# A new order in the state-space chunk, and D*u as diagonal matmuls on TensorE

## What is computed

```python
def _mamba(x, ...):
    xz = x @ in_w.T
    xi, z = jnp.split(xz, 2, axis=-1)
    xc = conv of 4 taps over time (xi)
    u = silu(xc + conv_b)
    x_dbl = u @ xproj_w.T                  # 16 columns dt, 16 B, 16 C
    delta = jax.nn.softplus(dt @ dt_w.T + dt_b)
    A = -jnp.exp(Alog)
    dA = jnp.exp(jnp.einsum('bld,dn->bldn', delta, A))
    dBu = jnp.einsum('bld,bln,bld->bldn', delta, Bm, u)
    def step(h, inputs):
        a, b, c = inputs
        h = a * h + b
        return (h, jnp.einsum('bdn,bn->bd', h, c))
    y = ys + u * Dp
    return y * jax.nn.silu(z) @ out_w.T
```

## Time and profile before

| | us |
|---|---|
| median of 3 runs | 8230.42 (8223.12 to 8230.87) |
| the profiled execution | 8213.02 |
| its span in the trace | 8211.7 |
| mean granted TensorE clock, share of full | 0.890 |

### The profile page before, as it was taken

One profiled execution on the slowest core, in us unless ns is written; L12 is line 12 of the kernel. 1 busy time (PEld: TensorE's weight loads), 2 busy tenths in 40 slices (PEclk: granted clock), 3 DMA queues, 4 the chain that ended last, 5 costly groups with the idle time before them and its releaser, 6 DMA issues. The chain is left out here.

```text
span 8211.7 us, 61601 instructions
## 1 busy us (share of the span) xinstructions
PE 6631.6 (81%) x19212; PEld 3520.3 (43%) x19212; DVE 6111.6 (74%) x7134; ACT 3152.1 (38%) x6327; POOL 3927.4 (48%) x2745
## 2 busy tenths in 40 slices
PE   5888878887788877888778888788887888878887
PEld 3533354333543335433354333543345443444433
DVE  6488965888658885588855888658886588765887
ACT  0255512554125541255412554134531355313553
POOL 3166541665425654255542655426543365433564
PEclk8889898898888988989989999898998988988998
DMA  2000010001100011000110001100001000110001
GB/s 77 19 29 28 27 47 13 29 31 39 32 19 24 31 39 40 13 24 29 39 40 13 29 24 39 40 13 31 24 36 40 16 29 26 36 37 16 29 29 36
DMA packets 211678, 248.50 MB, mean 30 GB/s; under 512 B 140858, under 2 KB 168546, under 8 KB 205412
## 3 DMA queue, kind: packets, MB, share of 16 engines
q1 hardware_dynamic: 211300, 244.04, 9.0%
HBM read 223.98 MB, written 20.03 MB: 30 GB/s over the span
## 5 line engine op out<-in xcount | busy, mean ns | idle before, releaser
L1142 DVE TENSOR_TENSOR_SCAN wk<-ps,wk 128x1024 f32<-128x1024 f32 x1024 | 2333.6, 2280 | 267.9 <-POOL wk L1697 139.6
L1364 PE MATMUL ps<-wk,ident 128*128 128x512 f32 x4096 | 2368.2, 707 | 101.0 <-DVE wk L1163 101.0
L1692 POOL TENSOR_TENSOR wk<-wk 128x1024 f32<-128x1024 f32 x1024 | 2403.2, 2357 | 8.6
L1606 ACT ACTIVATE ps<-wk,Aneg 128x255 f32<-128x255 f32 x4096 | 1700.8, 462 | 1569.2 <-DVE wk L1142 1520.0
L1354 PE MATMUL ps<-wk,ident 48*128 48x256 f32 x2048 | 767.2, 457 | 909.2 <-DVE wk L1151 857.8
L1151 DVE TENSOR_TENSOR wk<-wk,ps 128x1024 f32<-128x1024 f32 x1024 | 1224.9, 1196 | 92.2 <-issue 37.4
L1364 PEld LDWEIGHTS ps<-wk,ident 128*128 128x128 f32 x4096 | 781.2, 211 | 1066.0 <-issue 1063.7
L403 POOL TENSOR_SCALAR rstd<-mv 128x4 f32<-128x4 f32 x146 | 36.1, 247 | 2342.8 <-DVE mv L396 2342.8
L1354 PEld LDWEIGHTS ps<-wk,ident 48*128 48x128 f32 x2048 | 320.6, 196 | 1394.0 <-DVE wk L1151 1243.6
L509 POOL TENSOR_TENSOR wk<-wk 128x4096 f32<-128x4096 f32 x64 | 529.4, 8278 | 294.6 <-ACT wk L631 294.6
L1645 POOL TENSOR_TENSOR wk<-wk 128x1024 f32<-128x1024 f32 x64 | 150.4, 2350 | 1067.1 <-ACT wk L1531 1067.1
(11 more groups left out here) (175 smaller groups left out, 7495.8 us busy)
## 6 DMA issues: line engine op xcount, KB each, us to landing
wk<-bc_scr SPq DMA_DIRECT2D x256, 512.0 KB, 3.6
wk<-in_wgT SPq DMA_DIRECT2D x8, 1536.0 KB, 6.6
wk<-in_wuT SPq DMA_DIRECT2D x8, 1536.0 KB, 9.6
wk<-in_wdn SPq DMA_DIRECT2D x8, 1536.0 KB, 6.5
wk<-in_x SPq DMA_DIRECT2D x18, 512.0 KB, 4.0
o_scr<-wk SPq DMA_DIRECT2D x64, 128.0 KB, 3.0
wk<-o_scr SPq DMA_DIRECT2D x32, 256.0 KB, 3.5
wk<-wf_scr SPq DMA_DIRECT2D x8, 1024.0 KB, 4.8
```

Source lines behind the costliest of these rows:

```text
L1142: V.tensor_tensor_scan(h, in_time(d, flat(decay(m))), h, 0.0, ALU.mult, ALU.add).then_inc(scanned, 1)
L1364: mm = nc.tensor.matmul(bank(j), ident[:], hc[m % RC][:, 2 * j:2 * j + 2, :].rearrange("p e t -> p (e t)"), start=(n == 0), stop=(n == DS ...
L1606: nc.scalar.activation(decay(m)[:, e, rest(d)], dl[g % 2][:, e, rest(d)], ACT.Exp, scale=Aneg[:, d, e, n:n + 1]).then_inc(dA_done, 1)
L1692: nc.gpsimd.tensor_tensor(hb[n], du[g % 2], col(Bb[j % 2][:, n % NB, :]) .broadcast_to([P, NDI, MC]), ALU.mult).then_inc(dbu, 1)
```

## The change

- The D*u term: `Ddiag` holds, made once, a 128 x 128 diagonal matrix of D for each direction and tile. PE adds D*u in four f32 matmuls (`through`) to the running sums at step 1 of the chunk itself. The four multiply-adds of `finish` go.
- The rows of C: POOL cuts the C part of x_dbl into three bf16 parts (`part_c`, five operations), which lie on separate partitions since `xpT` now repeats the C columns (112 output rows for 48). `weights` is one bf16 matmul with a selection column `sel3`, and waits for `c_part`.
- The order: `project` goes to steps 4 to 7 in quarters, and both 128-token halves are evacuated by one DVE operation at step 9. The dt product is done in two double pieces at steps 2 and 3. The softplus parts go to steps 8 to 11 on ACT and 10 on DVE. On POOL, `part_c`, `lost`, `delta` and `du` of the next chunk come after all 16 inputs of the present one. The exponential for the carried state goes from step 0 to step 13 of the chunk before. The layer norms of half 1 start at step 10 of chunk 6 and end in chunk 7.
- Once per run: `xpT` is zeroed by POOL and loaded in six transfers for one, and `Ddiag` and `sel3` are made on DVE. The work area is 4 KB per partition smaller and some buffers move.

The core of the diff:

```diff
@@ -36,6 +36,8 @@
...
 XP = DTR + 2 * DS
+XC = (DTR + DS, 64, 96)
+XR = XC[-1] + DS
 HF, RANK = 1024, 16
...
@@ -83,7 +85,8 @@
...
         inT = sb("inT", [P, 2, KC, 2 * DI])
-        xpT = sb("xpT", [P, 2, NDI, XP])
+        xpT = sb("xpT", [P, 2, NDI, XR])
+        sel3 = sb("sel3", [XR, DS], BF16)
         dtT = sb("dtT", [DTR, 2, DI])
...
@@ -238,6 +248,10 @@
...
                     sp.dma_start(dst[:], src.broadcast_to([P, src.shape[1]])).then_inc(loaded, 16)
+                sp.wait_ge(blank, 1)
+                for dst, src in SPREAD:
+                    for d in range(2):
+                        sp.dma_start(dst[:, d], src[:, d]).then_inc(loaded, 16)
                 sp.wait_ge(loaded, NLOAD)
...
@@ -280,6 +297,14 @@
...
                 nc.vector.memset(xnp[:, :, 0:PAD], 0.0).then_inc(padded, 1)
+                for d in range(2):
+                    for e in range(NDI):
+                        nc.vector.tensor_scalar(Ddiag[:, d, e, :], ident[:], Dp[:, d, e:e + 1], None, ALU.mult)\
+                            .then_inc(diag, 1)
+                nc.vector.tensor_tensor(half3, ident[0:XR, XC[0]:XC[0] + DS], ident[0:XR, XC[1]:XC[1] + DS],
+                                        ALU.add).then_inc(picked, 1)
+                dve.wait_ge(picked, 1)
+                nc.vector.tensor_tensor(sel3[:], half3, ident[0:XR, XC[2]:XC[2] + DS], ALU.add).then_inc(picked, 1)
                 nc.vector.memset(xnp[:, :, PAD + T:], 0.0).then_inc(padded, 1)
...
@@ -760,17 +785,17 @@
...
             AHEAD = {X: 2, XD: 1, LG: 1, Z: 1}
-            PRE_PE = {0: (XD, 0), 3: (LG, 0), 4: (LG, 1), 5: (LG, 2), 6: (LG, 3), 8: (X, 0), 9: (X, 1), 10: (X, 2),
+            PRE_PE = {0: (XD, 0), 2: (LG, 0), 3: (LG, 1), 8: (X, 0), 9: (X, 1), 10: (X, 2),
                       11: (X, 3), 12: (Z, 0), 13: (Z, 1), 14: (Z, 2), 15: (Z, 3)}
-            Z_ACT, XD_ACT, LG_ACT = {0: 0, 1: 1, 2: 2, 3: 3}, 3, {7: 0, 8: 1, 9: 2, 10: 3}
-            OUT_PE, OUT_DVE = {1: 0, 2: 1}, {3: 0, 4: 1}
-            XN_PE = {7: (0, 0), 8: (0, 1), 9: (1, 0), 10: (1, 1)}
-            XN_ACT = {11: (0, 0), 12: (0, 1), 13: (1, 0), 14: (1, 1)}
+            Z_ACT, XD_ACT, LG_ACT = {0: 0, 1: 1, 2: 2, 3: 3}, 4, {6: 0, 7: 1}
+            OUT_PE, OUT_DVE = {4: (0, 0), 5: (0, 1), 6: (1, 0), 7: (1, 1)}, 9
+            XN_PE = {8: (0, 0), 9: (0, 1), 10: (1, 0), 11: (1, 1)}
+            XN_ACT = {12: (0, 0), 13: (0, 1), 14: (1, 0), 15: (1, 1)}
...
-                if g and n in OUT_PE:
-                    return OUT, g - 1, OUT_PE[n]
+                if g and n == min(OUT_PE):
+                    return OUT, g - 1, 0
                 if g == NU - 1 and n in XN_PE:
...
@@ -790,13 +815,14 @@
...
             CONV = {10: 0, 11: 1, 12: 2, 13: 3}
-            SOFT = {10: "abs", 11: "exp", 12: "ln", 13: "less"}
-            SILU, SUM = 15, 13
-            POOL_PRE = {13: ("lost",), 14: ("delta", "du")}
-            CLOSE_DVE = {5: ("stats0",), 7: ("apply0", "stats1"), 9: ("apply1",), 11: ("stats2",), 14: ("apply2",)}
-            CLOSE_POOL = {7: "rstd0", 10: "rstd1", 12: "add", 13: "rstd2"}
+            SOFT = {8: "abs", 9: "exp", 10: "ln", 11: "less"}
+            SILU, SUM, INJ, DIRECT = 15, 10, 13, 1
+            NPART = 2 * PARTS - 1
+            CLOSE_DVE = {10: ("stats0",), 12: ("apply0", "stats1"), 14: ("apply1",), DS + 1: ("stats2",),
+                         DS + 4: ("apply2",)}
+            CLOSE_POOL = {DS + 1: "add", DS + 5: "rstd2"}
             CLOSE_UNIT = NU - 2
...
@@ -1155,18 +1181,16 @@
...
                         dve.wait_ge(sig, DS * (g + 1))
-                        for e in range(NDI):
-                            V.scalar_tensor_tensor(out=y[:, e, :], in0=u_[g % 3][:, e, :], scalar=Dp[:, d, e:e + 1],
-                                                   in1=y[:, e, :], op0=ALU.mult, op1=ALU.add).then_inc(fin, 1)
                         dve.wait_ge(silu_z, g + 1)
-                        dve.wait_ge(fin, NDI * (g + 1))
                         V.tensor_tensor(z, y, z, ALU.mult).then_inc(gated, 1)
-                    def out_evac(g, t):
+                    def out_evac(g):
                         d, c = UNITS[g]
-                        dve.wait_ge(out_mm, g * MT + t + 1)
-                        y = ytok[:, c * MT + t, :]
-                        V.tensor_tensor(y, out_slot(g, t), pb[:] if d == 0 else y, ALU.add).then_inc(out_ev, 1)
+                        dve.wait_ge(out_mm, g + 1)
+                        y = ytok[:, c * MT:(c + 1) * MT, :]
+                        V.tensor_tensor(y, out_slot(g).rearrange("p (a c) -> p a c", c=C),
+                                        col(pb[:]).broadcast_to([P, MT, C]) if d == 0 else y, ALU.add)\
+                            .then_inc(out_ev, 1)
...
@@ -1200,7 +1224,7 @@
...
                     dve.wait_ge(e_xn_ready, 3 * KC)
-                    dve.wait_ge(pre_ev, 1 + 2 * NDI)
+                    dve.wait_ge(pre_ev, len([p for p in FLAT if p in PLACE]))
                     for i in range(2):
...
@@ -1217,26 +1241,24 @@
...
                                 finish(g - 1)
-                            if g and n in OUT_DVE:
-                                out_evac(g - 1, OUT_DVE[n])
+                            if g and n == OUT_DVE:
+                                out_evac(g - 1)
                             if g + 2 < NU and n in CONV:
...
                                 softplus(g + 1)
-                            if g == CLOSE_UNIT:
-                                if n == min(CLOSE_DVE):
-                                    dve.wait_ge(out_ev, MT * g)
-                                for name in CLOSE_DVE.get(n, ()):
-                                    close_step(1, name, 0, 0)
+                            if m == CLOSE_UNIT * DS + min(CLOSE_DVE):
+                                dve.wait_ge(out_ev, g)
+                            for name in CLOSE_DVE.get(m - CLOSE_UNIT * DS, ()):
+                                close_step(1, name, 0, 0)
                     weigh(DS * NU - 1)
...
                         square(s)
-                    for t in range(MT):
-                        out_evac(NU - 1, t)
+                    out_evac(NU - 1)
                     squares = iter(range(UP_FIRST, NF))
-                    dve.wait_ge(out_ev, MT * NU)
+                    dve.wait_ge(out_ev, NU)
                     for name in ("stats0", "apply0", "stats1", "apply1", "stats2", "apply2"):
...
@@ -1308,30 +1328,32 @@
...
                             for e in range(NDI):
-                                mm = nc.tensor.matmul(o[0:XP, :], xpT[:, d, e, :], u_[g % 3][:, e, :], start=(e == 0),
+                                mm = nc.tensor.matmul(o[0:XR, :], xpT[:, d, e, :], u_[g % 3][:, e, :], start=(e == 0),
                                                       stop=(e == NDI - 1))
                         else:
-                            mm = nc.tensor.matmul(o, dtT[:, d, i * P:(i + 1) * P], xd[g % 2][0:DTR, :], start=True,
-                                                  stop=True)
+                            for e in range(2):
+                                mm = nc.tensor.matmul(o[:, e * MC:(e + 1) * MC],
+                                                      dtT[:, d, (2 * i + e) * P:(2 * i + e + 1) * P],
+                                                      xd[g % 2][0:DTR, :], start=True, stop=True)
                         mm.then_inc(pre_mm, 1)
-                    def project(g, t):
+                    def project(g, t, half):
                         d, c = UNITS[g]
-                        if t == 0:
+                        if (t, half) == (0, 0):
                             pe.wait_ge(gated, g + 1)
-                        if g < NU - 1:
-                            take_slot((OUT, g, t))
-                        o = out_slot(g, t)
-                        for e in range(NDI):
+                            if g < NU - 1:
+                                take_slot((OUT, g, 0))
+                        o = out_slot(g)[:, t * C:(t + 1) * C]
+                        for e in (2 * half, 2 * half + 1):
                             mm = nc.tensor.matmul(o, sz[g % 2][:, e, t * P:(t + 1) * P], WcT[:, d, e, :],
...
                             t0 = c * MC + t * P
-                            for k in range(KC):
-                                mm = nc.tensor.matmul(o, xnT[:, k, t0:t0 + P], PxT[:, k, :], start=False,
-                                                      stop=(k == KC - 1))
-                        mm.then_inc(out_mm, 1)
+                            mm = nc.tensor.matmul(o, xnT[:, half, t0:t0 + P], PxT[:, half, :], start=False,
+                                                  stop=(half == 1))
+                        if (t, half) == (MT - 1, 1):
+                            mm.then_inc(out_mm, 1)
...
@@ -1347,11 +1369,10 @@
...
                         if n == 0:
-                            pe.wait_ge(pre_ev, evacuated((XD, g, 0)))
```

(58 more changed lines are left out.)

71 lines of the change are left out of this document (41 added, 30 removed).

## The result

The changed kernel takes 7576.6 us (median of four runs, 7576.4 to 7579.5), the kernel before 8226.8 in runs beside it (8214.0 to 8230.9). The ratio is 0.9213, with a 95% interval of 0.9197 to 0.9229: 650 us less, where 517 were forecast (7713). The time lies 23 us under the low end of the range, 7600. The nearest case is rival A, 7605, in which the waits go and PE's clock costs nothing; the result is 28 us under that too.

The account below looks back on a forecast made before the run. DVE was taken to set the pace of the state-space stage, losing its waits; 8213 - 113 - 25 - 5 - 210 - 208 - 70 + 32 + 78 + 5 = 7697 us, scaled to the median 7713, range 7600 to 7900.

Parts of the forecast that it names:

- rival A: State-space stage: the waits go entirely, PE keeping its clock, without +32 and +78; 7587, median about 7605; chance 0.15.
- D*u on PE: Four multiply-adds per chunk leave DVE, 113 us less; PE's added matmuls cost nothing, up to 121 us without cover.
- Waits for the D*u operations: DVE's 45.0 us of waits before the D*u operations: 25 us less, bounds 0 to 45.
- The projection: Quarters at steps 4 to 7, one evacuation: waits before evacuations 210 us less, their work 5 less.
- +32: Forward chunks: last projection quarter about 1 us late for DVE's evacuation, 32 us more, bounds 0 to 80.
- The order on POOL: All 16 scan inputs before the next chunk's softplus: DVE's waits before scans 208 us less, nothing late instead.
- Rival D: DVE's period stays, for instance since POOL beside it slows it; only 113 us gained, about 8115; chance 0.03.
- The C rows in bf16: Shorter C rows let PE catch up: DVE's 92.2 us of waits before weighings fall by 70, bounds 40 to 90.
- Layer norms: Layer norms of half 1 move into chunks 6 and 7: nothing, 0 to 3 us x 8.
- PE's clock: More half-clock stretches in steps 10 to 14, 1.4 us per chunk: 78 us more, bounds 0 to 224.
- Preparation: Once per run, six transfers for one and eight small products on DVE: 5 us more, 0 to 15.

## Why the prediction was wrong in size and right in mechanism

By its own steps, forecast first:

1. *D*u on PE*, -113: right. The undo costs 112. "At nothing" for PE was right only in this order: without the split projection it costs 63 us of new wait, about half of the 121 us named as its bound.
2. *Waits for the D*u operations*, -25: 45.0 + 6.7 became 17.3 before the gating, -34.
3. *The projection*, -210 and -5, with +32 for an evacuation that is late: the waits are 220.8 - 19.8 = 201 less, the work 10.5 less. What is left is the tail of each stage (17.1 in 8 waits, 2.1 each for 1.30), so that inside the stages every evacuation is in time. **The +32 was the first mis-sized term: it measured nothing**; the 32 evacuations of the forward direction wait 2.6 us in all. Its working added a row of 0.3 us, a sum of 1.82 and a quarter of 1.34 (which make 3.46, and were put at 3.4) against 3.31, and let the delay of the D*u matmuls pile up. The 0.3 was taken near the length of a record, and records of neighbouring matmuls overlap. From start to start the row is 0.12, and the sum behind it 1.72. With 1.47 for the quarter the step is 3.31. PE just keeps up.
4. *The order on POOL*, -208: 267.9 - 59.5 = 208.4. The C parts take 2.8 us (3 forecast), and neither delta nor the exponential is late. What the sum didn't have is that POOL's softplus operations now stand beside DVE's mask and layer norm. The layer-norm product went from 43.3 us busy (its group in the profile before) to 61.3, +18. The mask went from 89.2 to 101.1, which 11 us less of wait for ScalarE made good. Rival D named that mechanism and dismissed it by the scans, which are the operations that don't show it.
5. *The C rows in bf16*, -70 at the weighings: 92.2 became 10.4, -82. Its larger effect was booked elsewhere: without it the quarters of point 3 don't fit, and the undo costs 245.
6. *Layer norms*: no new wait; the +18 of busy time is under 4.
7. *PE's clock*, +78: **the second mis-sized term, and the larger one. It measured nothing** (the waits before the convolutions are 111.3 for 113.5, and only 2.5 of them inside the chunks, for 18.3 before; ahead of the stages, which the term didn't count, they are 108 for 95, the clock being lower there in more stages). The lower clock was really there, 0.80 to 0.84 in the convolution steps of chunk 1. Two steps of the working failed. It doubled the sum, the row and the X piece together, near 6 us, where the half clock covered only the sum (3.37, then the piece at full rate, 4.57 in all), so that it fitted into 5.3. And it took the turn of the chunk for 3 us late at half clock, where the clock was 1.00. The bound "from 0" was right and the value of 1.4 us per chunk a guess between bounds. The extra-work runs put the edge: 1.86 us more in three steps a chunk costs 33 us, 3.60 costs 146.
8. *Preparation*, +5: the first scan starts at 416.68 for 416.55. Nothing.

So the gap between forecast and result is 7713 - 7577 = 136 us. 16 of them are the scaling from the profiled run to the median, which the changed kernel doesn't have (its profiled run is its median). The other 121 are the positive terms of 32, 78 and 5, and 12 + 9 + 5 by which points 5, 2 and the evacuations' work were put too low, less 18 for POOL's interference and some 7 for longer tails. That is 116; 5 are spread over small groups. Without +32 and +78 the sum is rival A's 7605, whose mechanism was the right one and whose price was 28 us too high, by the scaling and the smaller terms just named; that is why even the range that began at A's end did not hold the result. A had been given 0.15, on the argument that the trace of before showed slow clocks. That trace showed how often the clock falls, not whether the step it falls on has room. The room could have been read from it: 5.3 us of a convolution step less 0.62, 1.82 and 0.95 for row, sum and piece is 1.9, and a sum at half clock takes up 1.8.

The Trainium skill, TensorE: Matmul & The Clock Gate, What's actually happening, ties the clock to how busy PE has recently been, and the prediction read it as a rule against taking work from PE. It didn't go that way: the mean granted clock rose from 0.890 to 0.906, though PE lost 723 us of busy time and its share of the span fell from 81% to 78%. In the chunk it is 0.95 at 53.55 of 65.60 us (82%); the same chunk of the kernel before had 0.89 at 65.60 of 78.90 (83%). The mean share doesn't tell the two apart; where PE idles does. Work added in the convolution steps alone raised the mean from 0.907 to 0.917 (four matmuls) and 0.928 (eight), and in chunk 1 the clock is 1.00 in steps where it was 0.80 to 0.84. Bringing back DVE's wait for POOL, by the old softplus order, lowered it to 0.893, which fits idle time of PE at that wait but was not taken apart further. The rule isn't contradicted; my use of it, less work and so a lower clock, was wrong here.

What the undos say together: D*u 112, order 244, projection 341, rows 245 make 942 us, for a total gain of 616 on these chips (8195.6 - 7579.6). The parts condition one another, so a share of the gain for each can't be given. The negative terms of the prediction came out within some 12 us each because they priced the waits, each of which is one number in the trace, and not the edits.

## What to carry to other kernels

Where one engine sets the pace and the waits are known, sum the waits; then test each neighbour's step by start-to-start times, not by record lengths, against the pace, because here a row of 0.12 or 0.63 us decided between nothing and 245 us. A lower clock costs only what exceeds the slack of the step on which it falls, so compute that slack before giving the clock a price. When the pacing engine has no wait left in a stretch, only work taken off it makes that stretch shorter, and the first and last pass through a stage must be priced apart from the steady state.

## What the hardware showed that was not expected

- VectorE operations with both tensor inputs in SBUF nearly stand still beside a two-input operation of GpSimd: 1.21 us alone, 2.80 and 3.25 beside one, ending 1.09 us after it in both cases and 1.07 to 1.10 after it in all 56 sums that met one in the run with the whole projection, and the GpSimd operation itself took 2.75 for 2.36. Four layer-norm products took 6.00 us beside three GpSimd operations (the line below is from the changed kernel), where half of all such products in the run take 0.48 us or less each. Scans and weighings with an input in PSUM were not slower. The Trainium skill, GPSIMD Engine Reference, Specifications, says that GpSimd shares its SBUF interfaces with VectorE and contends with VectorE instructions that have two SBUF inputs; the runs agree, and put the size to it.

```profile
858.80 6.00 DVE L446 SCALAR_TENSOR_TENSOR ytok<-ytok,mv,lnw 128x256 f32<-128x256 f32 x4
```

- A broadcast row of 256 columns held TensorE 0.12 us in bf16 and 0.63 in float32, and the float32 sum behind it 1.72 and 1.82. The ratio is 5, not the 2.5 that the record lengths (0.28 and 0.70) suggest.
